# A fused two-layer attention kernel: four of a step's eight transposes placed between its value matmuls

## The reference

```python
# layer 0
scores = einsum('bcn,bcm->bnm', theta, phi)
attn = softmax(scores, axis=-1)
y = einsum('bnm,bcm->bnc', attn, g).reshape(B, C, H, W)
z = (1 - w) * x + w * conv1x1(y, wz_w, wz_b)
# layer 1, with z as its x
att = softmax(einsum('bdi,bdj->bij', q, k) / sqrt(d_k), axis=-1)
out = gamma * einsum('bcj,bij->bci', v, att)
fused = einsum('oc,bchw->bohw', Wf, concatenate([out, z], axis=1)) + bf
```

## Time and profile before

| | us |
|---|---|
| median of 3 runs | 558.24 |
| lowest, highest | 557.75, 558.55 |
| span of the profiled execution | 556.1 |
| median less span | 2.1 |
| PE busy in it | 533.2 |
| DVE busy | 432.3 |
| ACT busy | 372.2 |
| POOL busy | 303.1 |

### The profile page before, as it was taken

One profiled execution on the slowest core, in us unless ns is written; L12 is line 12 of the kernel. 1 busy time (PEld: TensorE's weight loads), 2 busy tenths in 40 slices (PEclk: granted clock), 3 DMA queues, 4 the chain that ended last, 5 costly groups with the idle time before them and its releaser, 6 DMA issues.

```text
span 556.1 us, 9700 instructions
## 1 busy us (share of the span) xinstructions
PE 533.2 (96%) x2933; PEld 463.9 (83%) x2933; DVE 432.3 (78%) x633; ACT 372.2 (67%) x668; POOL 303.1 (55%) x288
## 2 busy tenths in 40 slices
PE   7898999999999999999999999999999999899996
PEld 6878787887889888898888988889788998787886
DVE  5947687688787887878877888778887786989973
ACT  5655567567784667657777486765867647778773
POOL 1565257684276742865448752578516681274442
PEclk9999999999999999999999999999999999999999
DMA  3010000001000010001000010000100000000011
GB/s 115 1 38 2 0 1 0 2 2 58 0 21 0 18 38 0 19 0 57 0 0 19 0 57 0 0 19 0 57 0 0 19 1 19 1 2 18 3 39 38
DMA packets 4630, 9.21 MB, mean 17 GB/s; under 512 B 896, under 2 KB 1408, under 8 KB 4608
## 3 DMA queue, kind: packets, MB, share of 16 engines
q1 hardware_dynamic: 4464, 8.80, 4.7%
q10 hardware_dynamic: 144, 0.13, 0.1%
HBM read 4.74 MB, written 4.19 MB: 16 GB/s over the span
## 4 chain that ended last, share of the span: by engine, by line
PE 80%; DVE 7%; ACT 6%; issue 5%; POOL 1%; DMA 1%; ACTq 0%; DVEq 0%
PE trans L485 17%; PE accum L509 9%; PE accum L511 9%; PE accum L510 9%; PE scores L450 5%; PE scores L475 5%; PE scores L451 4%; PE scores L452 4%; PE misc L450 3%; PE misc L452 3%; PE misc L451 3%; PE misc L536 3%; ACT probs L621 2%; DVE pt_lo L753 2%; ACT pt_hi L630 2%
## 5 line engine op out<-in xcount | busy, mean ns | idle before, releaser
L753 DVE TENSOR_TENSOR pt_lo<-trans,pt_hi 128x512 fp32r<-128x512 f32 x256 | 164.6, 685 | 56.4 <-ACT pt_hi L630 54.9
L630 ACT ACTIVATE pt_hi<-trans 128x512 fp32r<-128x512 f32 x256 | 139.7, 597 | 79.2 <-PE trans L485 77.9
L743 DVE TENSOR_REDUCE neg_max<-scores 128x1 f32<-128x1024 f32 x128 | 155.7, 1216 | 2.2 <-PE scores L452 1.3
L621 ACT ACTIVATE probs<-scores,neg_max 128x1024 f32<-128x1024 f32 x128 | 143.8, 1124 | 4.2 <-DVE neg_max L743 3.8
L485 PE MATMUL trans<-ident,probs 128*128 128x128 f32 x1024 | 135.5, 275 | 10.9 <-DVE pt_lo L753 7.2
L485 PEld LDWEIGHTS trans<-ident,probs 128*128 128x128 f32 x1024 | 115.0, 141 | 26.1 <-DVE pt_lo L753 8.4
L450 PE MATMUL scores<-phi_hi,theta_hi 128*128 128x512 f32 x112 | 57.0, 509 | 0.1
L509 PE MATMUL accum<-pt_hi,g_hi 128*128 128x512 f32 x136 | 54.4, 400 | 0.0
L510 PE MATMUL accum<-pt_lo,g_hi 128*128 128x512 f32 x136 | 53.5, 394 | 0.0
L511 PE MATMUL accum<-pt_hi,g_lo 128*128 128x512 f32 x136 | 53.4, 393 | 0.0
L858 POOL TENSOR_TENSOR theta_hi<-proj_full,zero 128x512 fp32r<-128x512 f32 x14 | 14.5, 1038 | 60.2 <-ACT proj_full L649 60.2
(11 more groups left out here) (161 smaller groups left out, 1067.6 us busy)
## 6 DMA issues: line engine op xcount, KB each, us to landing
out_dram<-o_sb SPq DMA_DIRECT2D x15, 256.0 KB, 2.0
x_raw<-x_dram SPq DMA_DIRECT2D x7, 512.0 KB, 3.6
x_raw<-x_dram SPq DMA_DIRECT2D x2, 256.0 KB, 3.7
w_all<-weights_t_dram SPq DMA_DIRECT2D x1, 336.0 KB, 3.8
out_dram<-o_sb SPq DMA_DIRECT2D x2, 128.0 KB, 1.9
w_all<-weights_t_dram ACTq DMA_DIRECT2D x1, 128.0 KB, 3.8
g_bias_rows<-g_bias_dram SPq DMA_DIRECT2D x1, 64.0 KB, 3.4
col<-columns_dram SPq DMA_DIRECT2D x1, 2.5 KB, 3.1
```

Of the source, the lines that this page charges most:

```text
L621: nc.scalar.activation(probs[:, k % 2, :], scores[:, k % 2, :], ACT.Exp, bias=neg_max[:, k % 4:k % 4 + 1], accum_out=row_sum[:, slot(gb), ...
L630: nc.scalar.activation(pt_hi[:, gb % 2, 4 * bank:4 * bank + 4, t * P:(t + 1) * P], trans[:, cols(bank)].rearrange("p (n q) -> p n q", n=4) ...
L743: nc.vector.tensor_reduce(neg_max[:, k % 4:k % 4 + 1], scores[:, k % 2, :], AX.X, ALU.max, negate=True).then_inc(max_ready, 1)
L753: nc.vector.tensor_tensor(pt_lo[at], trans[:, cols(bank)].rearrange("p (n q) -> p n q", n=4), f(pt_hi[at]), ALU.subtract).then_inc(pt_lo_r ...
```

## The change

`values_among_transposes` takes the place of `value_chunk` and `unit_transposes` in each step that has exactly one value chunk, is between 2 and 128, and whose chunk is not of the last block. These are steps 14 to 125, 112 of them. In the others PE's order is as before. In a changed step the after groups are issued first; then two value matmuls, the waits for probs and for bank 0 of trans, a transpose, and three more value matmuls each followed by a transpose; then the sixth value matmul, the wait for bank 1, and transposes 4 to 7. The other engines' programs are the same.

```diff
+            def values_among_transposes(gb, c, k, it):
...
+                for i in range(6):
+                    n = 2 * c + i // 3
...
+                    last = nc.tensor.matmul(accum[:, :], values, attention, start=(n == 0 and i % 3 == 0),
+                                            stop=(n == KT - 1 and i % 3 == 2))
+                    if i == 5:
+                        last.then_inc(pv_done, 1)
+                    if i == 1:
+                        pe.wait_ge(probs_ready, units(k, it))
+                        pe.wait_ge(pt_lo_ready, banks(k - 1, 0, it))
+                        turned(0)
+                    elif i == 2:
+                        turned(1)
+                    elif i == 3:
+                        turned(2)
+                    elif i == 4:
+                        turned(3).then_inc(trans_ready, 1)
+                pe.wait_ge(pt_lo_ready, banks(k - 1, 1, it))
+                for n in range(4, KT):
+                    last = turned(n)
+                last.then_inc(trans_ready, 1)
...
-                for gb in range(len(BLOCKS)):
-                    for c in range(CPB):
-                        if VALUE_STEPS[gb][c] == k:
-                            value_chunk(gb, c, it)
+                chunks_now = [(gb, c) for gb in range(len(BLOCKS)) for c in range(CPB) if VALUE_STEPS[gb][c] == k]
+                among = len(chunks_now) == 1 and 2 <= k <= UNITS and chunks_now[0][0] < len(BLOCKS) - 1
+                if not among:
+                    for gb, c in chunks_now:
+                        value_chunk(gb, c, it)
                 for group in after:
                     small(group, it)
-                if 0 <= k - 1 < UNITS:
+                if among:
+                    values_among_transposes(*chunks_now[0], k - 1, it)
+                elif 0 <= k - 1 < UNITS:
                     unit_transposes(k - 1, it)
```

More of the change, by code:

```diff
@@ L512, in value_chunk, with turned @@
                 last.then_inc(pv_done, 1)
+            def values_among_transposes(gb, c, k, it):
+                layer, b, h = BLOCKS[gb]
+                hi, lo = g_of(b) if layer == 0 else v_of(b)
+                if c == 0:
+                    pe.wait_ge(pt_lo_ready, banks(TPB * gb + TPB - 1, 1, it))
+                    pe.wait_ge(g_split if layer == 0 else v_split, halves(b, 1, it, 2))
+                    if gb:
+                        pe.wait_ge(accum_drained, blocks(gb - 1, it))
+                def turned(n):
+                    return nc.tensor.transpose(trans[:, n * P:(n + 1) * P], probs[:, k % 2, n * P:(n + 1) * P],
+                                               ident[:, :])
+                for i in range(6):
+                    n = 2 * c + i // 3
+                    tile = slice(n * P, (n + 1) * P)
+                    values = (hi, hi, lo)[i % 3][:, tile]
+                    attention = (pt_hi, pt_lo, pt_hi)[i % 3][:, gb % 2, n, :]
+                    last = nc.tensor.matmul(accum[:, :], values, attention, start=(n == 0 and i % 3 == 0),
[16 more added lines that the diff above has]
+                last.then_inc(trans_ready, 1)
             def small(group, it):
```

## The result

The changed kernel takes 634.53 us in the median of four runs (632.07 to 636.51) against 558.15 for the kernel before (four runs): 1.136 times as long, 95% interval 1.133 to 1.140. The forecast was 628 us in a range of 606 to 648. The profiled execution is the slowest of the four; its span is 634.7 us, 78.6 more than before.

The account below looks back on a forecast made before the run. The prediction took PE's issue to bound the kernel (busy 96% of 556.1 us). Part A +49.7, Part B +20.2, Part C +4.1 and Part D -4.0 gave +70.0 on 558.24: 628 us, range 606 to 648.

Parts of the forecast that it names:

- Part A: In steps with two small groups, the second and everything behind it on PE wait for the first's misc drain: +49.7 us.
- the hand-over from drain to PE: Time from the end of a misc drain to PE's next load, put at 0.05 to 0.06 us per stall.
- Part B: In short steps, the transposes' waits close a loop through ScalarE's exp and pt_hi copies that lengthens them: +20.2 us.
- The ring: Loop from exp through the eight transposes and the pt_hi copies to the next exp: 3.81 us, a floor for every step.
- from exp to the first transpose: Time from exp's start on ScalarE to the first transpose that waits for it: 1.26 us.
- Part C: Lone transposes among value matmuls cost 0.13 us each, +0.09 a step in layer 0 steps: +4.1 us.
- Part D: Step 28's wait for pt_lo behind a DVE cast shrinks as qk issues earlier: 0.8 us back, five times, -4.0 us.
- a clock under full: Sign against the forecast: a granted clock under full in the slices; the forecast had the clock unchanged.
- 1 (only the misc waits): Rival: the loop through ScalarE is slack and only Part A, Part C and Part D count: 608 us, chance 0.1.
- 2: Rival: weight loads hide behind transposes, a lone one costing 0.04 us: 593 us, chance 0.06.
- 4: Rival: not slower, the six drains are done in time and lone transposes cost 0.04 us: 528 us, chance 0.02.
- 3 (more than the sum, 649): Rival: ScalarE's and DVE's queues slip behind the stalls, another 0.3 us in 70 steps: 649 us, chance 0.12.

Follow-up runs that it names:

- late_two: The kernel changed only in the 70 steps without a second small group, with first transpose and both waits moved behind the fourth value matmul: 558.8 us, ratio 1.0008.
- layer0_quiet: Kernel before, changed only in 16 layer 0 steps with at most one small group, none following a qk group: 558.47 us, ratio 1.0003.
- no_doubles: Kernel before, changed only in the 70 steps without small groups both before and after: 579.88 us, ratio 1.039.

## Why the prediction was right

The direction, the two mechanisms and the sum held (+70.0 forecast, +76.4 measured). Step by step:

**Part A, right in mechanism, short by a tenth in the loop.** The period's six double steps cost 1.26, 1.36, 1.32, 1.28, 1.20 and 1.49, together 7.9, where 7.1 was forecast. The term that was mis-sized is the hand-over from drain to PE, put at 0.05 to 0.06. Rows of step 69 (g, then the z group, whose first operand is y_hi):

```profile
347.07 0.28 PE L572 MATMUL misc<-w_parts,x_hi 128*128 128x256 f32 x1
...
348.22 0.42 DVE L824 TENSOR_TENSOR values_full<-misc,values_full 128x256 f32<-128x256 f32 x1
...
348.77 0.19 PEld L450 LDWEIGHTS misc<-y_hi,w_parts 128*128 128x128 f32 x1 [1.28 <-issue]
348.77 0.49 PE L450 MATMUL misc<-y_hi,w_parts 128*128 128x512 f32 x1 [1.14 <-DVE values_full L824]
348.88 0.19 PEld L451 LDWEIGHTS misc<-y_lo,w_parts 128*128 128x128 f32 x1
...
349.11 0.39 PE L451 MATMUL misc<-y_lo,w_parts 128*128 128x512 f32 x1
```

The drain ends at 348.64. The first weight load and the first matmul both have 348.77 as their start, but this matmul is 0.49 long where the next is 0.39, and the next starts 0.34 behind it where 0.23 is the distance in a stream. So 0.11 of it is its own weight load, which in a stream is hidden. The load of the next weights, which goes with a matmul's start, says the same: it is at 348.88. From g's start to that it is 1.81, not 1.64. I had taken the distance to the weight load and not to the matmul. The load costs 0.11 behind each such stall (0.05 where the second group is y's transposes), and in three of the period's six the hand-over itself is 0.13 and not 0.06: 0.8 a period, and some 5 us over the 42.

**Part B, right in mechanism, short by a sixth in the loop.** The ring is 3.89 where 3.81 was forecast, read from two exps of short steps:

```profile
364.56 1.11 ACT L660 ACTIVATE probs<-scores,neg_max 128x1024 f32<-128x1024 f32 x1
...
365.89 0.33 PE L524 MATMUL trans<-ident,probs 128*128 128x128 f32 x1 [0.23 <-ACT probs L660]
...
367.29 1.27 ACT L669 ACTIVATE pt_hi<-trans 128x512 fp32r<-128x512 f32 x2 [1.53 <-PE trans L524]
367.33 0.60 PE L524 MATMUL trans<-ident,probs 128*128 128x128 f32 x4
...
367.68 0.71 PE L475 MATMUL scores<-k_op,q_op 96*128 96x512 f32 x2
...
368.46 1.11 ACT L660 ACTIVATE probs<-scores,neg_max 128x1024 f32<-128x1024 f32 x1
```

From exp to exp 3.90. Transpose 7 stands at 367.33 + 0.32 = 367.65, its copy begins 0.31 later (367.29 + 1.27 - 0.60 = 367.96), exp 0.50 after that: these were forecast as 0.31 and 0.48. From the first transpose to the eighth it is 367.65 - 365.89 = 1.76, as forecast. What is left is the term that was mis-sized, from exp to the first transpose: 365.89 - 364.56 = 1.33 where I had put 1.26. That 1.26 came from a row of the tail (471.71), and in the tail it still holds:

```profile
595.42 1.11 ACT L660 ACTIVATE probs<-scores,neg_max 128x1024 f32<-128x1024 f32 x1
...
596.67 0.33 PE L524 MATMUL trans<-ident,probs 128*128 128x128 f32 x1 [0.39 <-ACT probs L660]
```

There the short steps take 3.82. In the loop every transpose that waits for exp stands 1.32 to 1.34 behind its start; why, no run shows. Since the term is the ring less the step, 0.08 in the ring is much in it: the seven short steps of a period cost 3.80 and not 3.14, 19.0 us in five where 15.7 was forecast. The late_two kernel shows that the length of this ring is what costs: with 0.48 less of it, 21 of 29 us are gone. That layer 0 steps don't feel the wait was right but for step 46, which loses 0.3 to it.

**Part C was mis-sized.** Layer 0 steps with one group stayed where they were (step 77 at 4.54 us, step 78 at 4.64), and the transposes among value matmuls come at these starts:

```profile
383.77 0.61 PE L450 MATMUL scores<-phi_hi,theta_hi 128*128 128x512 f32 x1
...
386.58 0.27 PE L524 MATMUL trans<-ident,probs 128*128 128x128 f32 x1
...
386.93 0.27 PE L524 MATMUL trans<-ident,probs 128*128 128x128 f32 x1
...
387.96 0.60 PE L524 MATMUL trans<-ident,probs 128*128 128x128 f32 x4
388.31 0.61 PE L450 MATMUL scores<-phi_hi,theta_hi 128*128 128x512 f32 x1
```

A pair takes 386.93 - 386.58 = 0.35 to the rounding of the rows, and four pairs 387.96 - 386.58 = 1.38: 0.345 each, less 0.23 for the value matmul, 0.11 for the transpose, the same as its 0.107 in a run. I had taken 0.13, from the 0.31 behind y's transposes; that one gap doesn't carry over. The estimate that the prediction worked out from the Trainium skill, "TensorE: Matmul & The Clock Gate", section LDWEIGHTS (a load of 128 columns as P/1.2, 107 ns), was the 107 ns of a run, and the trace agrees. +4.1 became 0, as layer0_quiet confirms (ratio 1.0003, 0.9995 to 1.0012).

**Part D, right in sign, but not as I had it.** Step 28 lost 1.4 us in four of the five periods, not 0.8, and nothing in the first: 5.6 in all where 4.0 was forecast. Between nothing and 1.1 each was my range. The cast doesn't just come earlier: it now slips in ahead of GpSimd's x_lo and is over in 0.42 to 0.51, so the collision is gone rather than shortened. In the first period it started at 147.20, just behind x_lo at 147.14, and took 2.62. That this gain hangs on such an order, I had not seen, though both operations stood in the trace of the kernel before. Four gains beyond my range and one that is missing are not what I forecast, though the sum is near it.

**Not in the forecast: the clock.** I had expected it unchanged, and had named a clock under full as a sign against the forecast. That sign came. Windows of the changed kernel around step 18 (length, busy us and instructions of PE, PEld, DVE, ACT and POOL, then the granted clock, DMA share, GB/s):

```profile
97.00:98.00 1.00, 1.00 (x8) 0.86 (x7) 0.05 (x1) 0.39 (x1) 0.92 (x2) 0.99 0.00 0
98.00:100.00 2.00, 2.00 (x9) 1.46 (x8) 0.42 (x1) 0.00 (x0) 1.23 (x1) 0.50 0.00 0
100.00:101.00 1.00, 1.00 (x7) 0.82 (x5) 0.27 (x1) 0.60 (x1) 0.00 (x0) 0.50 0.00 0
101.00:102.00 1.00, 1.00 (x6) 0.88 (x5) 0.42 (x1) 0.62 (x2) 0.00 (x0) 0.81 0.00 0
```

From 98 to 101 us the granted clock is 0.50, the 1.2 GHz level. Step 18 takes 7.33 where steps 16, 17 and 19 take 5.36, 5.37 and 5.46. Step 111 takes 6.98, where it takes 5.62 with the groups first. In both places three stalls of 0.9 to 1.7 us had followed each other, and the clock was still full until 1.2 us after the last of them. The four runs show how much it makes: spans 634.7, 633.4, 632.0 and 630.3 at mean clocks of 0.994, 0.994, 0.997 and 0.999. That is up to 4.4 us of a run, some 2.5 of the median's 76, and most of the runs' scatter.

Of the rivals, 1 (only the misc waits) is refuted by no_doubles, 2 and 4 by the pairs above; 3 (more than the sum, 649) named the right sign of the remainder, but not its causes. That the sum came this close is in part luck: C's error (-4) and D's (-2) hid half of what A (some 5), B's loop (3), the clock (2.5) and step 14 (1.2, of which the forecast had nothing) were short.

## What to carry to other kernels

When an edit moves work past other work, price the moved waits before the moved instructions: here the title of the change names transposes, and their own price is nothing. The moved small groups, which lost the cover between two uses of one PSUM tile, make 45 us; the transposes' earlier wait for probs makes most of the other 31. A wait that moves ahead of independent work takes that work out of its shadow, and if it closes a ring with another engine, the way from the wait to the instruction that releases that engine sets the step. The same rule read backwards finds a gain: a group whose drain is late, issued before work that nobody waits for, made this kernel 1.5% faster than it was.

## What the runs showed of the hardware

- A DVE operation whose operands are all in SBUF was held off for as long as GpSimd's x_lo (two SBUF inputs, 128x1024, 2.4 us) ran, when x_lo had started first: beside it the cast took up to 2.65 us instead of 0.42, an addition of two SBUF inputs up to 2.5 instead of 0.68, and in the kernels looked at here each cast so held ended 0.27 to 0.29 after x_lo. A cast that started just ahead of x_lo took 0.42, and x_lo then 2.5 to 2.7. The same values from PSUM took 0.76 at all times, also wholly inside x_lo (step 15 above). The Trainium skill, "SBUF — State Buffer", section "SBUF: two separate sides", says that DVE and GpSimd share a pair of ports as an exclusive lock held for a whole instruction, and that DVE takes it in a 2-port mode or with two SBUF inputs. What the three forms did here agrees with that (which mode the cast runs in, no trace shows); my first theory, that only one-input operations are held, does not.
- After a stall PE's first matmul pays for its own weight load: it takes 0.34 us to the next start instead of 0.23 (348.77, 349.11), behind a hand-over of 0.05 to 0.13 from the drain's end.
- A transpose of 128 columns between matmuls of 512 columns costs 0.11 us (0.345 for the pair less 0.23), the same as in a run of transposes (0.107).
- The granted clock fell to 0.50 for about 3 us behind three PE stalls of 0.9 to 1.7 us, in two places of the changed kernel's trace, and behind a single one of 1.8 us in the kernel of layer 0 steps with one group, where four others of 1.7 to 1.95 us left it full. Executions of the same kernel differ in it (mean clock 0.994 to 0.999), and with the groups first, whose stalls are as many, the profiled run shows no fall. What decides that stays open.
